# Storing half of the destination one-hots of a graph network once and reading them back in its three recurrent layers

## What is computed

```python
# layer 0
messages = features[src]
h = segment_sum(messages, dst, num_segments=N)

# layer 2: a gated recurrent cell without history, three times (l = 0, 1, 2)
def gcn(x, W, b):
    xw = x @ W
    return segment_sum(nw[:, None] * xw[src], dst, num_segments=n) + b
I = sigmoid(gcn(x, W[0]) + ...); T = tanh(gcn(x, W[4]) + ...)
C = I * T
O = sigmoid(gcn(x, W[6]) + ... + wc * C)
out = O * tanh(C)
```

## Time and profile before

| | |
|---|---|
| median of three runs | 9894.26 us |
| the profiled execution: its own time | 9950.19 us |
| its span, first to last instruction | 9948.5 us |
| DVE busy | 6734.8 us (68%) |
| TensorE busy | 6270.1 us (63%) |
| ACT busy | 3919.7 us (39%) |
| GpSimd busy | 3064.5 us (31%) |
| bytes moved by DMA | 1158.29 MB |

### The profile page before, as it was taken

The page is one execution under the profiler, slowest core; times in us unless marked ns, Lnnn a source line. Parts: engine busy times, 40 slices in busy tenths (PEclk is TensorE's granted clock), DMA queues, the critical chain, the costliest instruction groups (busy, mean ns, idle before and its releaser), DMA issues. The chain is left out here.

```text
span 9948.5 us, 140910 instructions
## 1 busy us (share of the span) xinstructions
PE 6270.1 (63%) x41452; PEld 3103.4 (31%) x41922; DVE 6734.8 (68%) x11389; ACT 3919.7 (39%) x5017; POOL 3064.5 (31%) x2943
## 2 busy tenths in 40 slices
PE   3100120059878787978879787977777777455555
PEld 2100110025334333433334343433343434222222
DVE  8864650048778777877778787878897979533333
ACT  0000000012455554545545554544676757223223
POOL 0047437730233232323223232333000000455553
PEclk9999975579899898989989898988999999677777
DMA  2000000034667665766667676766211212101110
GB/s 80 3 13 1 4 22 9 5 91 140 211 202 227 203 218 196 229 204 209 217 198 233 201 225 198 228 199 194 67 58 61 64 52 64 20 18 25 22 21 24
DMA packets 493714, 1158.29 MB, mean 116 GB/s; under 512 B 115153, under 2 KB 150649, under 8 KB 492678
## 3 DMA queue, kind: packets, MB, share of 16 engines
q1 hardware_dynamic: 241952, 815.85, 25.7%
q10 hardware_dynamic: 157440, 298.89, 8.5%
q0 software_dynamic: 93568, 33.84, 2.7%
HBM read 932.28 MB, written 216.20 MB: 115 GB/s over the span
## 5 line engine op out<-in xcount | busy, mean ns | idle before, releaser
L1404 PE MATMUL acc<-dst_hot,parts 128*128 128x512 bf16 x11130 | 2918.2, 388 | 666.5 <-issue 430.2
L1463 ACT ACTIVATE parts_out<-acc 96x1024 bf16<-96x1024 f32 x2320 | 2339.9, 1020 | 2080.6 <-PE acc L1415 1773.9
L1367 POOL DMA_INDIRECT group_best<-best_dram,best_row x1250 | 1352.2, 1082 | 3079.7 <-SPq L1331 2775.3
L1279 DVE TENSOR_SCALAR dst_hot<-dst_rows,node_f 128x2048 bf16<-128x2048 int16 x2910 | 2052.1, 740 | 235.3 <-PE acc L1415 180.1
L1404 PEld LDWEIGHTS acc<-dst_hot,parts 128*128 x11600 | 1057.8, 99 | 1904.7 <-issue 804.7
L909 POOL DMA_INDIRECT gathered<-table_dram,source_index x719 | 729.4, 1014 | 2143.5 <-POOLq L153 1629.4
L304 POOL DMA_INDIRECT got<-edges_dram,record_index x928 | 952.7, 1027 | 850.1 <-DVEq L772 548.5
L1689 PE MATMUL sums_by_dst<-dst_hots,edge_message 128*96 128x512 bf16 x2436 | 879.6, 398 | 283.5 <-DVE dst_hots L1778 280.5
L1415 PE MATMUL acc<-source,parts 128*128 128x128 bf16 x9280 | 924.6, 223 | 8.8 <-issue 5.2
L1415 PEld LDWEIGHTS acc<-source,parts 128*128 x9280 | 642.0, 99 | 645.5 <-issue 380.9
L1778 DVE TENSOR_SCALAR dst_hots<-node_row,dst_col 128x640 bf16<-128x640 int16 x2436 | 794.7, 380 | 30.4
(11 more groups left out here) (373 smaller groups left out, 8030.9 us busy)
## 6 DMA issues: line engine op xcount, KB each, us to landing
dst_rows<-step_dst_dram SPq DMA_DIRECT2D x582, 512.0 KB, 5.2
source<-source_dram SPq DMA_DIRECT2D x582, 512.0 KB, 8.5
best_dram<-best_out ACTq DMA_DIRECT2D x580, 256.0 KB
factor<-step_weight_dram ACTq DMA_DIRECT2D x560, 256.0 KB
sources<-source_dram SPq DMA_DIRECT2D x174, 512.0 KB, 3.6
src_rows<-step_src_dram SPq DMA_DIRECT2D x58, 512.0 KB
source_dram<-source_made SPq DMA_DIRECT2D x58, 512.0 KB
group_best<-best_dram,best_row POOLq DMA_INDIRECT x1250
```

Of the source, the lines that this page charges most:

```text
L1279: nc.vector.tensor_scalar(hot[k % 2][b][:, :], index_rows[k % 3][:, :], node_f[:, b:b + 1], None, ALU.is_equal).then_inc(hot_ready, 1)
L1367: pool.indirect_dma_start(group_best[:, g, h, :], None, best_dram, bass.IndirectOffsetOnAxis(ap=best_row[:, i:i + 1], axis=0)).then_inc(en ...
L1404: nc.tensor.matmul(acc[n % 3][:, 0:TILE], blocks[b], hot[k % 2][b][:, q * TILE:(q + 1) * TILE], start=(b == 0), stop=(b == DST_BLOCKS - 1))
L1463: act.activation(moved[n % (2 * QUADS)][:, :], acc[n % 3][0:SPLIT, :], ACT.Copy).then_inc(tile_moved, 1)
```

## The change

Every other sub-tile (1, 3, 5 to 15: eight of a step, `KEPT_SUBS`) is kept. In the first layer DVE makes its one-hot into one of three buffers `dst_kept` of 128 x 8 x 640 bf16 (1.31 MB, 10240 bytes a partition) in place of the ring, and SP stores the buffer to `dst_hot_dram` when all one-hots of the step are made. In the recurrent layers SP reads it back into three buffers `dst_kept_in`, and TensorE takes the kept sub-tiles from there. ACT still makes two a step (now 6 and 14), DVE the remaining six (0, 2, 4, 8, 10, 12).

```diff
+KEPT_SUBS = tuple(range(1, STEP_SUBS, 2))
+MADE_SUBS = tuple(i for i in range(STEP_SUBS) if i not in KEPT_SUBS)
...
+    dst_hot_dram = nc.dram_tensor("dst_hot_dram", [STEPS1, P, len(KEPT_SUBS) * DST_NODES], BF16, kind="Internal").ap()
...
# first layer
+            dst_kept = [sb(f"dst_kept{i}", [P, len(KEPT_SUBS), DST_NODES], BF16, own) for i in range(3)]
+            def one_hot_of(n):
+                c, i = divmod(n, STEP_SUBS)
+                if i in KEPT_SUBS:
+                    return dst_kept[c % 3][:, KEPT_SUBS.index(i), :]
+                return dst_hot[(c * len(MADE_SUBS) + MADE_SUBS.index(i)) % HOTS1][:, :]
...
                 @block.sync
                 def _(sp):
-                    for k in range(STEPS1 + 1):
+                    for k in range(STEPS1 + 2):
...
-                        if k:
+                        if 1 <= k <= STEPS1:
                             c = k - 1
                             sp.wait_ge(source_ready, c + 1)
                             sp.dma_start(source_dram[c], source[c % 3][:, :]).then_inc(made_out[c % 3], 16)
+                        if k >= 2:
+                            c = k - 2
+                            sp.wait_ge(hot_ready, (c + 1) * STEP_SUBS)
+                            sp.dma_start(dst_hot_dram[c], dst_kept[c % 3][:, :, :].rearrange("p i n -> p (i n)")).then_inc(kept_out[c % 3], 16)
...
# first layer, DVE
                         for n in range(c * STEP_SUBS, (c + 1) * STEP_SUBS) if c >= 0 else ():
-                            if n >= HOTS1:
-                                dve.wait_ge(added, n - HOTS1 + 1)
-                            V.tensor_scalar(dst_hot[n % HOTS1][:, :], node_row[:, :], dst_col[:, n:n + 1], None, ALU.is_equal).then_inc(hot_ready, 1)
+                            i = n - c * STEP_SUBS
+                            if i == KEPT_SUBS[0] and c >= 3:
+                                dve.wait_ge(kept_out[c % 3], 16 * (c // 3))
+                                dve.wait_ge(added, (c - 2) * STEP_SUBS)
+                            r = c * len(MADE_SUBS) + MADE_SUBS.index(i) - HOTS1 if i in MADE_SUBS else -1
+                            if r >= 0:
+                                c_was, was = divmod(r, len(MADE_SUBS))
+                                dve.wait_ge(added, c_was * STEP_SUBS + MADE_SUBS[was] + 1)
+                            V.tensor_scalar(one_hot_of(n), node_row[:, :], dst_col[:, n:n + 1], None, ALU.is_equal).then_inc(hot_ready, 1)
...
# recurrent layers
-            ACT_SUBS = (7, 15)
-            DVE_SUBS = tuple(i for i in range(STEP_SUBS) if i not in ACT_SUBS)
+            ACT_SUBS = (6, 14)
+            DVE_SUBS = tuple(i for i in MADE_SUBS if i not in ACT_SUBS)
...
+            dst_kept = [sb(f"dst_kept_in{i}", [P, len(KEPT_SUBS), DST_NODES], BF16, own) for i in range(3)]
...
-                        for k in range(STEPS1):
-                            if k >= 3:
-                                sp.wait_ge(tile_found, (k - 2) * QUADS)
-                            sp.dma_start(source[k % 3][:, :], source_dram[k]).then_inc(source_in[k % 3], 16)
+                        for k in range(STEPS1 + 1):
+                            if k < STEPS1:
+                                if k >= 3:
+                                    sp.wait_ge(tile_found, (k - 2) * QUADS)
+                                sp.dma_start(source[k % 3][:, :], source_dram[k]).then_inc(source_in[k % 3], 16)
+                            if k:
+                                c = k - 1
+                                if c >= 3:
+                                    sp.wait_ge(added, (c - 2) * STEP_SUBS)
+                                sp.dma_start(dst_kept[c % 3][:, :, :].rearrange("p i n -> p (i n)"), dst_hot_dram[c]).then_inc(kept_in[c % 3], 16)
...
# recurrent layers, TensorE
-                                        if i in ACT_SUBS:
+                                        if i in KEPT_SUBS:
+                                            if i == KEPT_SUBS[0]:
+                                                pe.wait_ge(kept_in[c % 3], 16 * (c // 3 + 1))
+                                            one_hot = dst_kept[c % 3][:, KEPT_SUBS.index(i), :]
+                                        elif i in ACT_SUBS:
```

More of the change, by code:

```diff
@@ L1076, in _ @@
                         sp.wait_ge(made_out[i], 16 * len(range(i, STEPS1, 3)))
+                        sp.wait_ge(kept_out[i], 16 * len(range(i, STEPS1, 3)))
                 @block.tensor
@@ L1140, in _ @@
                                     pe.wait_ge(hot_ready, n + 1)
-                                    nc.tensor.matmul(to[0], found[c % 2][:, i, :], dst_hot[n % HOTS1][:, 0:BANK], start=False, stop=False)
-                                    nc.tensor.matmul(to[1], found[c % 2][:, i, :], dst_hot[n % HOTS1][:, BANK:DST_NODES], start=False, stop=False).then_inc(added, 1)
+                                    nc.tensor.matmul(to[0], found[c % 2][:, i, :], one_hot_of(n)[:, 0:BANK], start=False, stop=False)
+                                    nc.tensor.matmul(to[1], found[c % 2][:, i, :], one_hot_of(n)[:, BANK:DST_NODES], start=False, stop=False).then_inc(added, 1)
                                 if m + 1 < TILES:
@@ L1590, in program @@
                 with phase("vec", "weights_in", "bias_ready", "source_in0", "source_in1", "source_in2", "tile_found", "tile_moved", "found_used",
-                           "weighed_ready", "part_ready", "message_ready", "hot_ready", "far_ready", "act_hot_ready", "added", "closed", "flat_ready", "gates_done", "act_done", "out_ready", "out_done") as (
+                           "weighed_ready", "part_ready", "message_ready", "hot_ready", "far_ready", "act_hot_ready", "added", "closed", "flat_ready", "gates_done", "act_done", "out_ready", "out_done", "kept_in0", "kept_in1", "kept_in2") as (
                         block, vec, weights_in, bias_ready, source_in0, source_in1, source_in2, tile_found, tile_moved, found_used,
-                        weighed_ready, part_ready, message_ready, hot_ready, far_ready, act_hot_ready, added, closed, flat_ready, gates_done, act_done, out_ready, out_done):
-                    source_in = (source_in0, source_in1, source_in2)
+                        weighed_ready, part_ready, message_ready, hot_ready, far_ready, act_hot_ready, added, closed, flat_ready, gates_done, act_done, out_ready, out_done, kept_in0, kept_in1, kept_in2):
+                    source_in, kept_in = (source_in0, source_in1, source_in2), (kept_in0, kept_in1, kept_in2)
                     WEIGHTS_IN = 16 * (len(GATES) * 6 + 1)
@@ L1771, in hot_subtile @@
                         def hot_subtile(c, i):
-                            if c < 0 or i in ACT_SUBS:
+                            if c < 0 or i not in DVE_SUBS:
                                 return
```

5 lines of the change are left out of this document (3 added, 2 removed).

## The result

The changed kernel takes 10044.3 us (median of four runs, 10025.6 to 10091.3), the kernel before, run beside it, 9878.1: a ratio of 1.0172, interval 1.0143 to 1.0201. That is 166 us slower, where 178 us faster was forecast. The profiled execution took 10091.3 us, span 10089.6.

The account below looks back on a forecast made before the run. DVE was taken to bound the recurrent layers. Their -191 us and the first layer's +13 made -178, from 9950.2 us profiled to 9772, or 9716 against the median of 9894.3; range 9600 to 9860.

Parts of the forecast that it names:

- the walk round the ring: Recurrent layers: following the waits among DVE, TensorE and ACT once round gave 7.1 us a step for 8.21, -191 us.
- at about 6.77: Recurrent step: TensorE finds tile 3 at about 6.77 us after the second cast, copy 2 having started at 6.25.
- DVE is the bound, and the others follow it: Recurrent layers before the change: DVE, busy 269.86 of 300 us, sets the 8.21 us step; TensorE and ACT wait.
- First layer: After the gathers: the store ahead of the index row lengthens the step from 6.5 to 6.75 us, +13 us.
- Rival D: First layer: the store fills the DMA engines, at 200 GB/s a 10 us step, total 10095 us; chance 0.09.
- The transfers of the recurrent layers: Recurrent layers: kept loads take 4.3 us at 305 GB/s, 6.0 us of DMA in a 7.1 us step, hidden.
- C: Loads at 243 GB/s make recurrent steps 7.2 to 7.7 us, first-layer store up to 75 us: 9790 to 9880; chance 0.22.
- E: Recurrent layers: TensorE waits for kept loads as long as it did for DVE, no gain, 9895 us; chance 0.06.
- Rival B: Recurrent layers: TensorE's floor of 6.24 us sets the step, -343 us, total some 9565 us; chance 0.13.
- stage 4 some 7.1 us apart: Sign of a right forecast: in the recurrent layers, DVE's stage 4 starts some 7.1 us apart.
- DMA at 255 GB/s: Sign of a right forecast: DMA share near 0.8 at some 255 GB/s in the recurrent layers.
- no wait for the kept load: Sign of a right forecast: in the recurrent layers, TensorE does not wait for the kept load.

Follow-up runs that it names:

- e3: The changed kernel with DVE's one-hots 10 and 12 made right after 8, ahead of stage 4: 8671.6 us, ratio 0.9796 to the kernel before.
- e4: The changed kernel with 55 of 58 kept loads left out in each recurrent layer (sums of other destinations): ratio 1.0094 to the kernel before.
- e13: Kernel before with the first-layer store, issued one SP loop later than in the change, and 54 steps gathered ahead: first-layer tile 2.04 us.
- e14: As e13, but TensorE's queue makes one register load for the whole first layer (wrong rows): first-layer tile 1.54 us.
- e9: Kernel before with the first-layer store, 54 steps gathered ahead and one register load for the whole first layer (wrong rows): 9932.0 us.
- e10: Kernel before, without the store, with 54 steps gathered ahead and one register load for the whole first layer: 9828.6 us.
- e15: The changed kernel with no one-hots on ACT, eight on DVE (10 ahead of stage 4), store one loop later: 8521.1 us, ratio 0.9614.
- e2: Kernel before with the changed first layer's kept buffers, but without the store and the wait for it: ratio 1.0020.
- e12: The kernel of e3 run again on the slower kind of chip: 9853.8 against 9932.4 us for the kernel before, ratio 0.9904.

## Why the prediction was wrong

**Recurrent layers: forecast 7.1 us a step and -191 us, measured +71 us.** The step that failed is the walk round the ring. It followed DVE from stage 7 to one-hot 4 and ACT through its two blocks to the casts, and then had TensorE find tile 3 "at about 6.77" as soon as ACT had copied tile 2. Between the two stand sub-tiles 8 to 11, and one-hot 10 lies behind stage 4 on DVE, as one-hots 0, 2 and 4 lie behind the stages that I did count. Walked with the durations of before, from cast to cast: stage 4 after 0.65, one-hot 10 after 0.60 more, TensorE 0.43, tile 3 found 0.68 later (7306.26 to 7306.94), tile 0 of the next loop 1.56 later, its copy 0.4, and two blocks of 1.92: 8.2 us.

That this is the step of the kernel before is no chance: the same ring set it there. In the earlier trace rows it can be followed once round. The first cast starts at 7208.88, stage 4, which stands for it, at 7209.53, one-hot 10 at 7210.14, TensorE, which stands for that, at 7210.57; it finds tile 3 at 7211.25 and tile 0 of the next loop at 7212.81, and on ACT it goes on without a gap to the next cast:

```profile
7213.23 0.49 ACT L1746 ACTIVATE found<-rows_found 128x384 bf16<-128x384 f32 x1 [1.12 <-PE rows_found L1671]
7213.62 0.82 ACT L1727 ACTIVATE dst_far<-node_row,dst_col 128x640 bf16<-128x640 int16 x1
...
7217.10 0.61 ACT L1721 ACTIVATE edge_message<-weighed 128x512 bf16<-128x512 f32 x1
```

Cast to cast is 8.22 us, and in 43 steps of that layer in a row each goes the same way, in 8.18 to 8.35 us. So "DVE is the bound, and the others follow it", the first reading of the prediction, was wrong as well: DVE was busy 90% of the time, but its stall of 0.65 us before stage 4 was the ring showing. Only stage 4 and one-hot 10 of DVE's work lie in this ring, and none of the one-hots that the change takes away does. The change gains nothing, therefore, until e3 takes the one link out and finds 7.08 us; the sum of all other terms of the walk was right. What e3's order would have given in the kernel before, without any stored one-hots, was not tried.

That the recurrent layers came out 71 us slower, and not merely unchanged, is the clock. In the three layers of the changed kernel 89 of 171 steps are 8.6 to 9.6 us long, 9.1 in the mean, and nearly all the others 8.2 to 8.3, as before. The longer ones are those with matmuls of 0.63 us, and what grows in them is TensorE's way from tile 3 to tile 0 and the copy behind it (1.6 and 0.4 us, then up to 2.5 and 0.6):

```profile
7253.47 0.69 DVE L1831 TENSOR_TENSOR weighed<-weighed,edge_message 128x512 f32<-128x512 f32 x1 [3.36 <-ACT edge_message L1757]
7261.67 0.69 DVE L1831 TENSOR_TENSOR weighed<-weighed,edge_message 128x512 f32<-128x512 f32 x1 [2.45 <-ACT edge_message L1757]
7271.06 0.69 DVE L1831 TENSOR_TENSOR weighed<-weighed,edge_message 128x512 f32<-128x512 f32 x1 [3.36 <-ACT edge_message L1757]
```

(8.20 and 9.39 us.) Before, TensorE's gaps were at most 1.1 us in one piece and the clock stayed at 1.00; now it stands 1.9 us once a step, then runs partly at 1.2 GHz and is at 0.89 in the mean. The prediction had put nothing down for the clock. That the gap lowers the clock is the likely reading, since e3 removes both and e4, without the loads, keeps both; it was not tried apart.

**First layer: forecast +13 us, measured +88.** The term was built on the index row's landing and on the DMA engines' rate. Both were sized tolerably (the row was late 24 us in 290; the engines went up to 396 GB/s where I took 420), and neither was what bound. What bound was an instruction that the prediction never named, the register load on TensorE's queue, stretched from 0.31 to 0.75 us while the stores run: 0.43 us a tile, 232 tiles less the 26 under the gathers, 0.43 x 206 = 89 us. That these loads held the tile is shown by e13 and e14 together; but the other two terms stood so close behind them that taking the loads out alone gave back nothing of the store's price (e9 and e10). Rival D had the right stage and sign but the wrong resource: the loss came at a rate of 295 GB/s and more, far above the 230 from which D was to decide.

The DMA engines moved 396 GB/s in the mean of 300 us in e14. The Trainium skill, "DMA: Bandwidth & Descriptors", section Specifications, has a limit of about 358 GB/s to HBM for one core; these runs don't agree with it, and what the layer lost was lost well below it, at 295.

**The transfers of the recurrent layers** were right: a kept load lands after 5.6 us (median of 174), TensorE never waits for it, and e4 shows that leaving it out changes nothing. Rivals C and E fall. **Rival B,** TensorE's floor of 6.24 us, was right as a floor: e15 reaches it with ACT's one-hots out of the ring. **Signs:** "stage 4 some 7.1 us apart" (8.2 to 9.6), DMA at 255 GB/s (210) and "no wait for the kept load" were the right things to look at, and the first two failed together, as they must.

## What to carry to other kernels

An engine that is busy 90% of the time and still stands once a step need not be the bound: follow that one wait back, from releaser to releaser, until it comes round to itself, and if the loop adds up to the step, the loop is the bound, and only work that lies in it is worth taking away. Where engines wait for each other in a fixed order, walk the ring through **every** instruction that stands behind a waiting one on its queue, to the last consumer of the step; work that waits for nothing belongs ahead of the wait. Before adding bulk stores to a stage, look for small synchronous reads on a compute queue there: they have no share in the busy columns, and here they stretched to 0.75 us from 0.31 at a DMA share of 0.86.

## What the runs showed of the hardware

- A register load of TensorE's queue from SBUF takes 0.30 us with DMA at 168 GB/s, 0.74 in the mean and up to 1.84 with 1.31 MB stores beside it at 296 GB/s. In the recurrent layers, where the bulk goes from memory into SBUF, the 696 loads stay at 296 to 328 ns (median 301) at 210 GB/s, and at 293 to 327 (median 300) in e15 at 285 GB/s: it goes with the stores of 1.31 MB and not with the rate. Four registers in one load take 0.99 us at least.
- Contiguous traffic in both directions reached 396 GB/s in the mean of 300 us, at a full share (e14).
- The same kernel took 8855 us on one kind of chip and 9900 on another. The difference lies in the stages in which GpSimd issues gathers: in the first layer TensorE made 2436 matmuls in 600 us on the one (e2), 228 in 630 us on the other (the kernel before), while the recurrent layers of one kernel (e3, e12) take 1332 us on both. A change can be hidden on the one and exposed on the other.
- TensorE's granted clock was 1.00 in the kernel before, whose longest gap in a recurrent step was 1.1 us, and 0.89 in the changed one, where it stood 1.9 us once a step. That the gap is the cause was not tried apart.
